# A decoder layer on one core: zeros on TensorE before the first weights, the first rotary sums on VectorE, and the feed-forward parts dealt out anew between the last slots

## The reference

```python
x = _layernorm(x + attn(x, Wq, bq, Wk, bk, Wv, bv, Wo, bo))     # x: 16 x 256 x 512
x = _layernorm(x + _wkv(w, u, x, ctx_2048))
x = _layernorm(x + ffn(x, W, bias, rw1, rb1, rw2, rb2, A, B, gates))
```

## Time and profile before

| | us |
|---|---|
| median of 3 runs (1618.47 to 1620.61) | 1619.72 |
| the profiled execution, its own time | 1619.31 |
| its span, first to last instruction | 1617.5 |
| TensorE busy | 1554.8 |
| VectorE busy | 1341.2 |
| ScalarE busy | 1117.2 |
| GpSimd busy | 1013.3 |

### The profile page before, as it was taken

How to read it: one execution, slowest core, us unless ns; L and a number is a source line. 1 busy time by engine, 2 the same in 40 slices (tenths; PEclk the granted TensorE clock), 3 DMA queues, 4 the chain that set the end, 5 groups by cost and what they waited for, 6 DMA issues and landing times.

```text
span 1617.5 us, 32631 instructions
## 1 busy us (share of the span) xinstructions
PE 1554.8 (96%) x10464; PEld 1411.9 (87%) x10464; DVE 1341.2 (83%) x3431; ACT 1117.2 (69%) x2995; POOL 1013.3 (63%) x852
## 2 busy tenths in 40 slices
PE   7999999999999999999999999999999977989997
PEld 7899999999999999999999999999999866777885
DVE  6776698889888988898989898888988885867864
ACT  6877787877787778777877787878777764334332
POOL 3665586758675767576767676767676642735653
PEclk9999999999999999999999999999999998999999
DMA  8766344324442444244424442444244412121211
GB/s 291 249 215 217 112 141 147 112 73 152 143 131 65 146 149 136 55 149 147 137 59 151 151 137 60 151 151 137 60 147 153 142 51 86 53 87 70 79 66 52
DMA packets 81624, 202.61 MB, mean 125 GB/s; under 512 B 10416, under 2 KB 11056, under 8 KB 81456
## 3 DMA queue, kind: packets, MB, share of 16 engines
q1 hardware_dynamic: 81456, 200.53, 39.4%
HBM read 120.80 MB, written 37.75 MB: 98 GB/s over the span
## 4 chain that ended last, share of the span: by engine, by line
PE 80%; DVE 8%; issue 3%; POOL 3%; ACT 2%; DMA 1%; DVEq 1%; SPq 0%; ACTq 0%; POOLq 0%
PE bank L527 24%; PE bank L528 23%; PE bank L529 23%; PE bank L651 5%; PE bank L596 2%; PE bank L642 1%; PE bank L634 1%; PE bank L597 1%; DMA SW<-QB 1%; DVE PS L1302 1%; DVE QS L1295 1%; PE bank L666 1%; DVE ED L1313 1%; DVEq L1383 1%; DVE RC L1162 0%
## 5 line engine op out<-in xcount | busy, mean ns | idle before, releaser
L527 PE MATMUL bank<-Xh,W 128*128 128x256 f32 x1280 | 363.6, 284 | 10.8 <-DVE W L1405 7.2
L528 PE MATMUL bank<-Xl,W 128*128 128x256 f32 x1280 | 362.1, 283 | 0.0
L529 PE MATMUL bank<-Xh,W 128*128 128x256 f32 x1280 | 361.8, 283 | 0.0
L1019 POOL TENSOR_TENSOR Ql<-RC,Qh 128x512 fp32r<-128x512 f32 x128 | 170.1, 1329 | 213.0 <-ACT Qh L739 213.0
L754 ACT ACTIVATE S<-S,NM 128x128 f32<-128x128 f32 (+1 forms) x512 | 228.1, 447 | 66.4 <-DVE NM L1147 65.9
L527 PEld LDWEIGHTS bank<-Xh,W 128*128 128x128 f32 x1280 | 242.9, 190 | 13.6 <-DVE Xl L1208 7.2
L739 ACT ACTIVATE PTh<-bank 128x384 fp32r<-128x384 f32 x256 | 125.1, 489 | 173.6 <-PE bank L651 173.6
L1008 POOL TENSOR_TENSOR SW<-SW,tables 128x512 f32<-128x512 f32 x128 | 170.2, 1330 | 116.8 <-DMA SW<-QB 116.7
L528 PEld LDWEIGHTS bank<-Xl,W 128*128 128x128 f32 x1280 | 243.4, 190 | 0.0
L529 PEld LDWEIGHTS bank<-Xh,W 128*128 128x128 f32 x1280 | 243.3, 190 | 0.0
L739 ACT ACTIVATE S<-S,RL 128x128 f32<-128x128 f32 (+1 forms) x512 | 203.5, 447 | 31.5 <-DVE RL L1154 31.4
(11 more groups left out here) (155 smaller groups left out, 4446.6 us busy)
## 6 DMA issues: line engine op xcount, KB each, us to landing
W<-kept SPq DMA_DIRECT2D x140, 512.0 KB, 4.4
SW<-QB SPq DMA_DIRECT2D x256, 128.0 KB, 2.3
kept<-W SPq DMA_DIRECT2D x40, 512.0 KB, 4.7
XR<-XR SPq DMA_DIRECT2D x64, 128.0 KB, 2.3
RO<-in_xn SPq DMA_DIRECT2D x16, 512.0 KB, 4.0
KVT<-in_ctxt SPq DMA_DIRECT2D x16, 512.0 KB, 4.3
mixed<-RO SPq DMA_DIRECT2D x16, 512.0 KB, 4.0
XR<-in_xt SPq DMA_DIRECT2D x15, 512.0 KB, 5.1
```

The costliest lines, as they stand in the source:

```text
L527: nc.tensor.matmul(dst, lhs[0], rhs[0], start=first, stop=False)
L528: nc.tensor.matmul(dst, lhs[0], rhs[1], start=False, stop=False)
L529: return nc.tensor.matmul(dst, lhs[1], rhs[0], start=False, stop=last)
L1019: gp.tensor_tensor(Q[1][:, :, :], RC[:, i % 2, :, :], Q[0][:, :, :], ALU.subtract).then_inc(q_lo, 1)
```

## The change

There are three edits.

1. **Zeros.** GpSimd clears S[:, 0, 0:128] before anything else, and TensorE, ahead of its slots, runs 18 float32 matmuls of that tile with itself, 128 columns each, into the tails' bank. Nobody reads the result. GpSimd's memset now raises `consts` as well, so its two later waiters want 2.
2. **First sums.** For the first key tiles (s = 0) and the first pair of queries (i = 0) VectorE does what GpSimd did: KRC + KSW in slot 2, RC + SW and Ql in slot 3. GpSimd keeps the products with the sine.
3. **Dealing.** `FFN_SPLIT_AT` and the lists `PARTS_AT` and `PARTS` have other numbers. The work is the same, its place among the slots is not.

```diff
+FIRST_SUMS = [(2, 2), (3, 2), (3, 2)]
...
-FFN_SPLIT_AT = [254 + i for i in range(2 * KC + ER)]
+FFN_SPLIT_AT = [254, 254, 256, 257, 259, 260, 261, 262, 263, 264]
...
-PARTS = [2, 1, 1, 2, 2, 1, 2, 2, 1, 1, 2, 0, 1, 2, 1, 0, 1, 1, 1, 3, 1, 1, 2, 2, 0, 1, 1, 1, 0]
-PARTS_AT = {250: [(0, 0)], 257: [(1, 1)], 258: [(1, 2), (1, 0)], 262: [(2, 0)], 263: [(2, 1)], 264: [(2, 2)]}
+PARTS = [1, 1, 2, 3, 1, 1, 1, 2, 2, 0, 2, 0, 1, 1, 3, 1, 0, 2, 1, 3, 1, 1, 2, 1, 0, 1, 1, 1, 0]
+PARTS_AT = {250: [(0, 0)], 257: [(1, 1), (1, 2), (1, 0)], 262: [(2, 0), (2, 1)], 263: [(2, 2)]}
...
+            pe.wait_ge(consts, 1)
+            for _ in range(18):
+                nc.tensor.matmul(tail_ps[:, 0:P], S[:, 0, 0:P], S[:, 0, 0:P], start=True, stop=True)
             run(pe, slot, step=step)
...
-                    pool.wait_ge(consts, 1)
+                    pool.wait_ge(consts, 2)
...
-                    pool.wait_ge(q_cos, 2 * i + 2)
-                    pool.wait_ge(q_sin, i + 1)
-                    gp.tensor_tensor(RC[:, i % 2, :, :], RC[:, i % 2, :, :], SW[:, :, :], ALU.add).then_inc(q_summed, 1)
+                    if i > 0:
+                        pool.wait_ge(q_cos, 2 * i + 2)
+                        pool.wait_ge(q_sin, i + 1)
+                        gp.tensor_tensor(RC[:, i % 2, :, :], RC[:, i % 2, :, :], SW[:, :, :], ALU.add).then_inc(q_summed, 1)
...
-                if i is not None:
+                if i is not None and i > 0:
                     pool.wait_ge(q_hi, i + 1)
...
-                    pool.wait_ge(k_cos, JL * s + JL)
-                    pool.wait_ge(k_sin, s + 1)
-                    gp.tensor_tensor(KRC[:, :, :], KRC[:, :, :], KSW, ALU.add).then_inc(k_summed, 1)
+                    if s > 0:
+                        pool.wait_ge(k_cos, JL * s + JL)
+                        pool.wait_ge(k_sin, s + 1)
+                        gp.tensor_tensor(KRC[:, :, :], KRC[:, :, :], KSW, ALU.add).then_inc(k_summed, 1)
...
+            gp.memset(S[:, 0, 0:P], 0.0).then_inc(consts, 1)
             run(pool, slot, step=step)
...
+            def first_sums(n, place):
+
+                if (n, place) == FIRST_SUMS[0]:
+                    dve.wait_ge(k_cos, JL)
+                    dve.wait_ge(k_sin, 1)
+                    v.tensor_tensor(KRC[:, :, :], KRC[:, :, :], KSW, ALU.add).then_inc(k_summed, 1)
+                if (n, place) == FIRST_SUMS[1]:
+                    dve.wait_ge(q_cos, 2)
+                    dve.wait_ge(q_sin, 1)
+                    v.tensor_tensor(RC[:, 0, :, :], RC[:, 0, :, :], SW[:, :, :], ALU.add).then_inc(q_summed, 1)
+                if (n, place) == FIRST_SUMS[2]:
+                    dve.wait_ge(q_hi, 1)
+                    v.tensor_tensor(Q[1][:, :, :], RC[:, 0, :, :], Q[0][:, :, :], ALU.subtract).then_inc(q_lo, 1)
...
                 first_k_low(n)
+                first_sums(n, 2)
```

More of the change, by code:

```diff
@@ L1164, in cosines @@
                                            op0=ALU.add, op1=ALU.mult).then_inc(q_cos, 1)
+            def first_sums(n, place):
[10 more added lines that the diff above has]
+                    v.tensor_tensor(Q[1][:, :, :], RC[:, 0, :, :], Q[0][:, :, :], ALU.subtract).then_inc(q_lo, 1)
             def slot(n):
+                first_sums(n, 0)
                 inverses(n)
                 cosines(n)
+                first_sums(n, 1)
                 if n % 2 == 0:
@@ L1282, in tail @@
                         if tau == 0 and h == 0:
-                            dve.wait_ge(consts, 1)
+                            dve.wait_ge(consts, 2)
                             v.memset(A2Z[:, :, 0:1], 0.0)
```

## The result

The changed kernel takes 1607.30 us (median of 5 runs, 1603.67 to 1608.63), the kernel before, run beside it, 1620.61 (5 runs, 1618.47 to 1624.56). The ratio is 0.9909, 95% interval 0.9892 to 0.9925: 0.9% faster, 13.3 us by the medians and 14.7 by the ratio, where 7.2 were forecast. The profiled execution has a span of 1606.0 us against 1617.5, so the two traces are 11.5 us apart.

What follows compares the result with a forecast made beforehand. TensorE, busy 96%, bounds the kernel; its 60 to 1280 us cannot be shortened. Start 1.5, slots 257 to 264 4.0 and slots 273 to 276 1.5 sum to 7.0 off 1619.31: 1612.3, stated as 1612.5, range 1606 to 1617.

Steps and rivals of the forecast that it cites:

- The start, 1.5 us: First 60 us: zeros and first sums together gain 1.5 us, range -3 to 3.
- the 0.8 us carried from the zeros: Start: of 1.9 us gained on TensorE by the clock, 0.8 reaches Q1 and the first V tile.
- Ql's wait at 33.73: Start: TensorE's waits for Ql at 33.73 and 44.16 each come 1 to 2 us earlier.
- slots 257 to 264, 4.0 us: End: earlier turns and moved splits free OTl, gates and logits; 4.9 us worked out, 4.0 taken, ends 1.5 and 6.
- One sign: Experts' QB after slot 264: TensorE's 3.31 us wait falls by up to 1.7, at the first L701 below 2.
- Slots 273 to 276: Last tail: three waits of 2.27, 1.46 and 2.77 us shrink by 1.9 in sum; 1.5 taken, ends -1 and 3.5.
- The step that failed: Slots 278 to 288: TensorE's waits for GpSimd, 0.3 to 1.0 us a step, unchanged by the dealing; gain set at nothing.
- the rule for two weight splits at the start: Start: two-SBUF-input VectorE instructions and SBUF-reading GpSimd ones exclude each other; Vl 0 to 1.0 us earlier, 0.4 taken.
- the waits that the dealing was feared to shift: Rival, end: re-dealing only shifts waits, leaving 1.5 + 1.0 us of gain: 1617; chance 0.15 for 1616 to 1618.5.
- the overrun of the zeros: Rival, start: zeros outlast the first weights, at worst 1622.5; slower or level by overrun or new stalls, chance 0.07.
- the moment of the lower clock is not fixed: Rival: the clock's rise differs between runs, and low stretches fall differently; 1 to 2 us either way, 1611 to 1614.
- The case given 0.10: Whole kernel: more gained than counted, as in the upper ends 3 + 6 + 3.5, under 1608; chance 0.10.

Runs made afterwards that it cites:

- e3: The kernel before with zeros and first sums, parts dealt as before: 1618.15 us, ratio 0.9989 to the kernel before.
- e1: The kernel before with the zeros alone: 1619.18 us, ratio 0.9999 to the kernel before.
- e10: The changed kernel with FFN_SPLIT_AT as it was, all parts as changed: 1605.74 us, ratio 0.9920 to the kernel before.
- e13: The kernel before with part (3,2) moved from slot 266 to 267, behind the scans: 1616.98 us, ratio 0.9988.
- e16: The changed kernel with old FFN_SPLIT_AT, part (10,2) moved from slot 282 to 283, 8 products ahead of the last L701: 1607.52 us, ratio 0.9925 to the kernel before.

## Why the prediction was right and wrong

**The start, 1.5 us: the size right, by luck.** The mean over the traces is 1.5; the timings (e3, 0.9977 to 1.0001) cannot tell it from nothing. The zeros ran from 0.98 to 6.77 (forecast 1.2 to 7.8), 0.32 us a product on average, and the clock was up at the first real matmul. QB of head 3 came at 22.39 (22.8). But its division was off: the 0.8 us carried from the zeros do not last when they stand alone (in e1 the eleventh head's RC came 0.6 us later than before), and Ql's wait at 33.73 moved by 0.3, not 1 to 2; the one at 44.16 moved by 1.8.

**Right: slots 257 to 264, 4.0 us.** 3.7 by the means. The mechanism stands: no wait at the Wo of slot 259, the gate's wait at L713, and the gain grows as it was worked out: by the means of 7 and 9 kernels the Wo of slot 259 came 1.9 us earlier behind the RC of head 250 (forecast 2.0) and slot 265's products 2.7 (forecast 3.2). One sign was wrong: the first L701 waits 2.80 and not below 2, since GpSimd's four products took 3.82 us there (2.65 before). In the trace of the changed kernel alone this stretch gained only 2.1; it took nine traces to see 3.7. The parts' places gave it (e10), not the split slots.

**Slots 273 to 276: the waits right.** All three came out as forecast (2.27, 0.88, 1.43, against 2.27, 1.0 and 1.3), 1.9 us of idle time, for which I took 1.5. The length gained 2.6, but 0.8 of that is the wait of the seventh turn (1.23 us before, 0.46 after), which belongs to the next paragraph, and some 0.4 is work moved ahead of the fifth. That leaves about 1.4, an estimate from these numbers in a length that spreads by up to 5 us.

**The step that failed** is the last of the list: "The many small differences from 278 to 288 I set at nothing: TensorE waits there for GpSimd, 0.3 to 1.0 us a step, which the dealing does not change." Slots 265 to 273 had no term at all. The dealing does change it: how long GpSimd's gate takes depends on which VectorE instruction runs beside it, and the places of the parts decide that. I had used the rule for two weight splits at the start and did not ask it of the gate. The four products of one gate, from the first one's start to the last one's end, and TensorE's wait at the L700 (L701) behind them, counted as turns from the first one:

```
turn               2nd    3rd    7th    8th    9th    10th
gate, before       3.48   2.63   3.28   2.64   2.16   2.65
gate, after        1.62   1.65   1.79   1.64   3.48   1.65
wait, before       1.43   0.60   1.23   1.03   0.81   0.60
wait, after        0      0      0.46   0      1.61   0
```

Each gate length comes back within 0.03 us in every kernel with the same order at that place, and follows the order where kernels mix the two (only e16's moved ninth gate, 1.67, fits neither). With the fourth turn's, 0.54 and 0.26, these waits sum to 6.24 us before and 2.33 after, where the prediction let them stand. The forecast's error is of that size: 2.6 us by the means in slots 265 to 273, where e13 gets 1.9 by the ratio (0.3 to 3.4) with one part, 0.8 at the seventh turn, and 1.5 from there on. Of this last 1.5, 0.6 is how often the last step had the lower clock (6 of 8 old and 2 of 6 new), which is chance as far as these runs show; the waits of the eighth to tenth turn give 0.8. That a VectorE instruction beside the gate is what lengthens it was tested, by moving one part, for the second turn alone. For the third it is read from the trace of the kernel before (a scan of L1302 beside the second product, 1.40 us), for the seventh too (a scan of L1272 and an add of L1277 with both inputs in SBUF); for the eighth to tenth only the lengths show it.

The rivals: the waits that the dealing was feared to shift did not eat the gain, though the ninth turn's grew; the overrun of the zeros did not occur. That the moment of the lower clock is not fixed held, and it takes 1.6 us for one stretch in a step. The case given 0.10, more than I counted, is what happened (1607.3; the upper ends, 12.5 us, give 1607.2), through a cause it did not name. That 1607.3 lies within the range, near its edge, is so because the range was wide. The sum was also off by a little in itself: 1619.72 less 7.0 is 1612.7, not 1612.5.

## What to carry to other kernels

When parts are dealt anew among slots, list for each moved part what stands beside it on the engine that shares its SBUF access (VectorE for GpSimd), not only what stands ahead of it in its own queue: a GpSimd product that took 0.42 us took 1.4 beside a VectorE scan. Test one such move by undoing it alone. And where stretches of lower clock fall differently from kernel to kernel, compare a stretch over several traces; and before filling a wait to keep the clock, ask what TensorE will wait for next.

## What the runs showed of the hardware

- The collision goes both ways: GpSimd's products stretched from 0.42 to 1.40 us, and VectorE's scans from 1.22 and 1.24 to 1.72 and 2.25 beside GpSimd's tensor operations (e16).
- Float32 products of 128 by 128 ran in two records each, at 0.12 us a record at the full clock (24 in 2.84, 60 in 6.86) and 0.16 on average from a cold start (36 in 5.79).
- The granted clock stayed at 1.00 through both places where it had been 0.50, once TensorE multiplied in the wait ahead of them; behind the next wait, of 3.72 us, it was 0.50.
- The last wait of 2.4 us was followed by a lower clock in nine traces and not in seven, with the same work on both sides.
